# Cross-attention scores computed once with queries on partitions, tiles normalised by GpSimd and turned by TensorE transposes

## The reference

```python
q_r = jnp.einsum('bshq,hqr->bhsr', q_big, W_qr)
k_r = jnp.einsum('bld,hdr->bhlr', kv_rope, W_kr)
scores = jnp.einsum('bhsr,bhlr->bhsl', q_r, k_r)
attn = jax.nn.softmax(scores, axis=-1)
ctx_c = jnp.einsum('bhsl,bld->bhsd', attn, kv_rope)
ctx_lat = jnp.einsum('bhsd,hkd->bshk', ctx_c, w_kc_kv)
out = ctx_lat.reshape(b, s, H * K) @ Wo.T
```

## Time and profile before

| | |
|---|---|
| Median of three executions | 260.71 us (259.54 to 261.23) |
| The profiled execution | 261.54 us, of which the span of instructions is 259.4 us |
| Granted TensorE clock, mean | 0.983 |
| PE busy | 239.6 us, 92% of the span, 1563 matmuls |
| DVE busy | 196.5 us, 76% |
| ACT busy | 132.2 us, 51% |
| POOL busy | 103.3 us, 40% |
| Chain that ended last | PE 71%, DVE 13%, DMA 5%, ACT 4% |
| HBM read, written | 14.43 MB, 0.52 MB |

### The profile page before, as it was taken

How to read it: one execution, slowest core, us unless ns; L and a number is a source line. 1 busy time by engine, 2 the same in 40 slices (tenths; PEclk the granted TensorE clock), 3 DMA queues, 4 the chain that set the end, 5 groups by cost and what they waited for, 6 DMA issues and landing times.

```text
span 259.4 us, 4344 instructions
## 1 busy us (share of the span) xinstructions
PE 239.6 (92%) x1563; PEld 171.6 (66%) x1563; DVE 196.5 (76%) x351; ACT 132.2 (51%) x285; POOL 103.3 (40%) x135
## 2 busy tenths in 40 slices
PE   7999999988997799998999999999999999989971
PEld 4478797754654457675666767677776777668850
DVE  1377577899765899869889998986669895897574
ACT  1545377566368366556467656654435533313430
POOL 7297400000114307745466555556255533001362
PEclk9999999999999899999999999999999999999995
DMA  6999940000000840000000000000000000000011
GB/s 246 321 278 322 412 167 0 4 1 3 0 3 0 158 86 0 3 0 0 5 0 0 3 0 0 0 3 0 0 3 0 1 3 1 0 3 0 1 40 40
DMA packets 4500, 13.65 MB, mean 53 GB/s; under 512 B 512, under 2 KB 1280, under 8 KB 4352
## 3 DMA queue, kind: packets, MB, share of 16 engines
q1 hardware_dynamic: 4048, 11.29, 13.1%
q0 software_dynamic: 432, 2.10, 3.7%
HBM read 14.43 MB, written 0.52 MB: 58 GB/s over the span
## 4 chain that ended last, share of the span: by engine, by line
PE 71%; DVE 13%; DMA 5%; ACT 4%; issue 2%; SPq 2%; POOL 1%; POOLq 0%; DVEq 0%; ACTq 0%
PE ps L844 11%; PE ps L794 7%; PE ps L821 5%; PE ps L858 5%; PE ps L822 5%; PE ps L795 5%; PE ps L778 5%; DMA wq<-in_wq 5%; PE ps L634 3%; PE ps L923 3%; DVE mneg L1350 3%; PE ps L831 2%; PE ps L696 2%; PE ps L681 2%; PE ps L574 2%
## 5 line engine op out<-in xcount | busy, mean ns | idle before, releaser
L1184 ACT ACTIVATE probs<-ps 128x512 f32<-128x512 f32 x64 | 38.0, 597 | 46.7 <-PE ps L822 45.8
L1412 DVE TENSOR_REDUCE xmneg<-ps 128x1 f32<-128x512 f32 x64 | 43.0, 688 | 16.2 <-PE ps L795 15.8
L445 POOL TENSOR_TENSOR psums<-psums,probs 128x512 f32<-128x512 f32 x30 | 38.6, 1288 | 10.8 <-ACT probs L1184 8.3
L441 POOL TENSOR_TENSOR psums<-probs 128x512 f32<-128x512 f32 x15 | 19.2, 1281 | 43.1 <-ACT probs L1184 43.1
L794 PE MATMUL ps<-KA,QA 128*128 128x512 f32 x64 | 30.3, 474 | 2.8 <-DVE xmneg L1412 1.9
L844 PE MATMUL ps<-probs,kv_dup 128*64 128x256 f32 x256 | 31.2, 385 | 0.0
L1430 DVE RECIPROCAL xrcp<-ps 128x256 f32<-128x256 f32 x16 | 28.0, 1751 | 1.9 <-PE ps L831 1.9
L1176 ACT ACTIVATE QA<-ps 64x256 fp32r<-64x256 f32 x64 | 24.2, 378 | 10.1 <-PE ps L778 8.9
L1350 DVE TENSOR_REDUCE mneg<-ps 128x4 f32<-128x1024 f32 x16 | 19.6, 1224 | 9.4 <-PE ps L574 9.0
L821 PE MATMUL ps<-QA,KA 128*128 128x512 f32 x64 | 26.0, 406 | 0.0
L398 POOL TENSOR_TENSOR rstd<-mv,eps_col 128x1 f32<-128x1 f32 x12 | 2.3, 189 | 59.4 <-DVE mv L1338 59.1
(11 more groups left out here) (162 smaller groups left out, 459.7 us busy)
## 6 DMA issues: line engine op xcount, KB each, us to landing
wu<-in_wu SPq DMA_DIRECT2D x4, 640.0 KB, 8.9
wq<-in_wq SPq DMA_DIRECT2D x4, 512.0 KB, 13.4
wcT<-in_wcT SPq DMA_DIRECT2D x4, 384.0 KB, 12.3
wE<-in_wE SPq DMA_DIRECT2D x4, 320.0 KB, 11.2
w13T<-in_w POOLq DMA_DIRECT2D x1, 1024.0 KB, 8.2
x1T<-in_xT SPq DMA_DIRECT2D x1, 512.0 KB, 3.7
kvp<-in_kv POOLq DMA_DIRECT2D x1, 512.0 KB, 6.1
x_nat<-in_xn SPq DMA_DIRECT2D x1, 512.0 KB, 18.6
```

Of the source, the lines that this page charges most:

```text
L445: g.tensor_tensor(psums[:, s, :], psums[:, s, :], probs[:, s, kc, :], ALU.add).then_inc(xadd_sb, 1)
L1184: a.activation(probs[:, n % 2, kc, :], ps[:, 2 + u % 2, :], ACT.Exp).then_inc(xexp_sb, 1)
L1412: v.tensor_reduce(xmneg[:, n % 4, qt, hh:hh + 1], ps[:, u % 2, :], AX.X, ALU.max, negate=True).then_inc(xmax_sb, 1)
```

## The change

The scores are computed once, with queries on partitions. `xscores(n, r)` takes the place of both `xmax` and `xexp` on PE and uses banks 0, 1 and 2 in turn. DVE reduces each tile to its negated maximum as before; ACT then applies the exponential to the same tile with that maximum as a bias per partition, and gives the sum of each row as a second output (`xsum`). DVE takes the reciprocal of two columns of sums at a time, and POOL multiplies each 128x512 tile by it in place (`xnorm`, four per unit). PE transposes the tiles, four transposes of 128x128 for each block of keys (`xturn(t)`, t = 4m + kc, seven steps behind the scores: `OFF` = 7), into bank 3 for even t and bank 5 for odd t. ACT copies the even ones out of PSUM and DVE the odd ones, into `PT`, which lies where `probs` was. `xpv(m)` then runs all its eight matmuls in one piece, two iterations behind the scores, and DVE copies the result to `ctxn` (`context`). The sums by POOL, the matmul with ones, the split and transpose of the maxima, the rows they were copied to and the blanking of them are gone. The loop has still 18 iterations; `query(n + 2)` now stands in step r = 0. `routing(0)` moves behind the copies of step r = 2 of iteration 16. The diff, cut to its core (the new side mostly, since what is removed is described above):

```diff
+NQ = 3
+OFF = 7
+
+
+def score_bank(u):
+    return u % 2 if u < 4 else (u - 2) % 3
+
+
+LAST_IN_BANK = [max([w for w in range(u) if score_bank(w) == score_bank(u)], default=-1) for u in range(4 * NUNIT)]
...
+        PT = probs[:].rearrange("p s k q -> p (s k) q")
...
+        xmneg = sb("xmneg", [P, 3, 4], scope=late)
+        xsum = sb("xsum", [P, 3, 4], scope=late)
+        xrcp = sb("xrcp", [P, 3, 4], scope=late)
+        xp = sb("xp", [P, 3, 4, LK], scope=late)
...
+            pool.wait_ge(rstd_sb[0], 2)
+            g.memset(QB[DC:DC + 4].bitcast(F32), 0.0).then_inc(qzero, 1)
+            pool.wait_ge(qzero, 1)
...
+            def xnorm(n, r):
+                pool.wait_ge(xrcp_sb, 2 * n + r // 2 + 1)
+                g.tensor_scalar(xp[:, n % 3, r, :], xp[:, n % 3, r, :], xrcp[:, n % 3, r:r + 1], None, ALU.mult).then_inc(xnorm_sb, 1)
+
+            pool.wait_ge(const2, 2)
+            for n in range(NUNIT):
+                if n in (4, 5):
+                    reciprocal_root(0, n - 2)
+                if n in (NE + 5, NE + 6):
+                    reciprocal_root(1, n - NE - 5)
+                for r in range(4):
+                    xnorm(n, r)
...
-            def xmax(n, r):
+            def xscores(n, r):
                 b = n // NPAIR
                 hh, qt = r // 2, r % 2
                 u = 4 * n + r
                 s = n % NQ
                 if r == 0:
-                    pe.wait_ge(qzero, n + 1)
                     pe.wait_ge(qhi_sb, 4 * n + 4)
                     pe.wait_ge(qlo_sb, 2 * n + 2)
-                if u >= 2:
-                    pe.wait_ge(xmax_sb, u - 1)
...
+                if u == 0:
+                    pe.wait_ge(qzero, 1)
+                if u == 4:
+                    pe.wait_ge(exp_sb, 4 * NGRP)
+                if LAST_IN_BANK[u] >= 0:
+                    pe.wait_ge(xexp_sb, LAST_IN_BANK[u] + 1)
                 q = slice(qt * P, qt * P + P)
-                o = bank(u % 2)
+                o = bank(score_bank(u))
                 pe.matmul(o, QA[:, s, hh, q], KA[:, b * LK:(b + 1) * LK], start=True, stop=False)
...
+                pe.matmul(o, QB[:, s, hh, q], KB[:, b * LK:(b + 1) * LK], start=False, stop=True).then_inc(xs_ps, 1)
...
+            def xturn(t):
+
+                m, kc = t // 4, t % 4
                 if kc == 0:
-                    pe.wait_ge(xm_sb, 2 * n + 2)
-                if u == 0:
-                    pe.wait_ge(exp_sb, 4 * NGRP)
-                if u >= 2:
-                    pe.wait_ge(xexp_sb, u - 1)
-                k0 = b * LK + kc * P
-                o = bank(2 + u % 2)
-                pe.matmul(o, KA[:, k0:k0 + P], QA[:, s, :, :], start=True, stop=False)
-                pe.matmul(o, KB[:, k0:k0 + P], QB[:, s, :, :], start=False, stop=True).then_inc(xexp_ps, 1)
-
-            def xsum(n):
-
-                if n == NUNIT - 1:
-                    pe.wait_ge(xlast_sb, NKC - 1)
+                    pe.wait_ge(xnorm_sb, 4 * m + 4)
+                if t >= 2:
+                    pe.wait_ge(xT_dve if t % 2 else xT_act, t // 2)
+                for r in range(4):
+                    mm = pe.transpose(ps[:, 3 + 2 * (t % 2), r * P:(r + 1) * P], xp[:, m % 3, r, kc * P:(kc + 1) * P], ident[:])
+                mm.then_inc(xT_ps, 1)
+
+            def xpv(m):
...
+                b = m // NPAIR
+                pe.wait_ge(xT_act, 2 * m + 2)
+                pe.wait_ge(xT_dve, 2 * m + 2)
+                if m == 0:
+                    pe.wait_ge(sums_sb, NGRP)
                 else:
-                    pe.wait_ge(xadd_sb, 3 * n + 3)
-                for hh in range(2):
...
+                    pe.wait_ge(ctxn_sb, m)
+                for kc in range(NKC):
+                    for hh in range(2):
+                        mm = pe.matmul(ps[DC * hh:DC * hh + DC, 4, 0:SEQ], kv_dup[:, NKC * b + kc, 0, :],
+                                       PT[:, (4 * m + kc) % 8, hh * SEQ:(hh + 1) * SEQ], start=(kc == 0), stop=(kc == NKC - 1))
+                mm.then_inc(xpv_done, 1)
...
+                    t = 4 * n + r - OFF
...
                     if n < NUNIT:
-                        xmax(n, r)
-                    if LAG <= n < NUNIT + LAG:
-                        xexp(n - LAG, r)
-
+                        xscores(n, r)
+                    if r == 0 and n + 2 < NUNIT:
+                        query(n + 2)
...
+                    if n == NUNIT and r in (1, 2):
+                        for p in (2 * r - 2, 2 * r - 1):
+                            out_proj(2, p)
+                            out_proj(3, p)
+                    if n == NUNIT and r == 3:
+                        out_proj(2, 4)
+                        out_proj(3, 4)
                         gates_T(0, ps[:, 7, 0:SEQ])
-                    if n == NUNIT and r == 3:
+                    if n == NUNIT + 1 and r == 0:
+                        out_proj(2, 5)
+                        out_proj(3, 5)
                         spread_gates(0, 0)
                     if n == NUNIT + 1 and r == 1:
-                        out_proj(2, 4)
-                        out_proj(3, 4)
                         spread_gates(0, 1)
+                    if n == NUNIT + 1 and r == 2:
+                        out_proj(2, 6)
+                        out_proj(3, 6)
                     if n == NUNIT + 1 and r == 3:
-                        out_proj(2, 5)
-                        out_proj(3, 5)
                         spread_gates(0, 2)
...
+                    if r == 3 and n >= 2:
+                        xpv(n - 2)
+                    if 0 <= t < 4 * NUNIT:
+                        xturn(t)
+            up(0)
             spread_gates(0, 3)
-            for kc in range(NKC):
-                xpv(NUNIT - 1, kc)
-            xsum(NUNIT - 1)
-            out_proj(2, 6)
-            out_proj(3, 6)
-            up(0)
-            pe.wait_ge(xexp_sb, NKC * NUNIT)
...
+            def xexp(u):
+                n, r = u // 4, u % 4
+                act.wait_ge(xmax_sb, u + 1)
+                if r == 0 and n >= 3:
+                    act.wait_ge(xT_ps, 4 * (n - 2))
+                a.activation(xp[:, n % 3, r, :], ps[:, score_bank(u), :], ACT.Exp, bias=xmneg[:, n % 3, r:r + 1],
+                             accum_out=xsum[:, n % 3, r:r + 1]).then_inc(xexp_sb, 1)
+
+            def xturn(t):
+                act.wait_ge(xT_ps, t + 1)
+                if t == 0:
+                    act.wait_ge(pv_done, NGRP)
+                if t % 4 == 0 and t >= 8:
+                    act.wait_ge(xpv_done, t // 4 - 1)
+                a.activation(PT[:, t % 8, :], ps[:, 3, :], ACT.Copy).then_inc(xT_act, 1)
...
+                    u = 4 * n + r
+                    if 1 <= u <= 4 * NUNIT:
+                        xexp(u - 1)
...
+                    if r == 0 and n + 2 < NUNIT:
                         query_hi(n + 2)
...
+                    if n == NUNIT and r == 3:
                         gates_T(0, ps[:, 7, 0:SEQ])
+                    t = u - OFF
+                    if 0 <= t < 4 * NUNIT and t % 2 == 0:
+                        xturn(t)
...
-                hh, qt = r // 2, r % 2
...
+                dve.wait_ge(xs_ps, u + 1)
+                v.tensor_reduce(xmneg[:, n % 3, r:r + 1], ps[:, score_bank(u), :], AX.X, ALU.max, negate=True).then_inc(xmax_sb, 1)
+
+            def xrecip(n, k):
+                dve.wait_ge(xexp_sb, 4 * n + 2 * k + 2)
+                v.reciprocal(xrcp[:, n % 3, 2 * k:2 * k + 2], xsum[:, n % 3, 2 * k:2 * k + 2]).then_inc(xrcp_sb, 1)
+
+            def xturn(t):
+                dve.wait_ge(xT_ps, t + 1)
+                if t == 1:
+                    dve.wait_ge(pv_done, NGRP)
+                if t % 4 == 1 and t >= 8:
+                    dve.wait_ge(xpv_done, t // 4 - 1)
+                v.tensor_copy(PT[:, t % 8, :], ps[:, 5, :]).then_inc(xT_dve, 1)
+
+            def context(m):
+                b, p = m // NPAIR, m % NPAIR
+                dve.wait_ge(xpv_done, m + 1)
+                v.tensor_copy(ctxn[:, p, b * SEQ:(b + 1) * SEQ], ps[:, 4, 0:SEQ]).then_inc(ctxn_sb, 1)
...
+            for n in range(NUNIT + 2):
+                for r in range(4):
+                    t = 4 * n + r - OFF
+                    if n < NUNIT:
+                        xmax(n, r)
+                    if r == 0 and n >= 3:
+                        context(n - 3)
+                    if r == 0 and n in (NE + 5, NE + 6):
+                        norm_stats(1, n - NE - 5, ps[:, 7, 0:SEQ], x1)
+                    if r == 1 and 1 <= n <= NUNIT:
+                        xrecip(n - 1, 1)
+                    if r == 3 and n < NUNIT:
+                        xrecip(n, 0)
+                    if 0 <= t < 4 * NUNIT and t % 2 == 1:
+                        xturn(t)
+                    if r == 2 and n < 3:
+                        attn_norm(NGRP - 3 + n)
+                    if r == 2 and n in (4, 5):
+                        norm_apply(0, n - 2, x1)
+                    if r == 2 and n in (NE + 5, NE + 6):
```

(13 more changed lines are left out.)

230 lines of the change are left out of this document (23 added, 207 removed).

## The result

The change makes the kernel slower, and by more than forecast. The median goes from 260.91 us (259.54 to 261.23, four executions) to 281.41 us (280.06 to 283.28, four executions); the ratio is 1.081 with a 95% interval of 1.077 to 1.085. The prediction was 265 us, with a range that ended at 270.

What follows compares the result with a forecast made beforehand. The prediction took a PE-DVE loop to bound full units at 8.0 us against 7.42. Its stretches, +4.5 - 1.6 + 3.5 - 2.0 + 0.4 - 0.7, gave +4.1 and a median of 265 us, range 258.5 to 270.

Steps and rivals of the forecast that it cites:

- the loop: Units of the main loop: PE and DVE wait for each other once a unit, 8.0 us against 7.42 before.
- the small reciprocal: DVE's reciprocal of 128x2 sums: taken as 0.20 us, between 0.17 and 1.10.
- the exponential: ACT's exponential with bias column and row sum: taken as 0.87 us in all, range 0.68 to 1.28.
- PE's saving: PE's own work per unit about 1.1 us below 7.42; comes through in units 12 and 13, -2.0 us.
- the wait at `gates_T`: After unit 16 starts, `gates_T` waits for `routing(0)` on DVE behind the copy of step 2: 2.4 us stall.
- Rivals 1, 2 and 3: PE-DVE loop shorter, 260 us (chance 0.16); loop doesn't close, 252 us (0.05); loop longer, 269 us (0.13).
- rival 4: PE's clock falls to 0.50 in the loop, if transposes don't count as busy: above 315 us, chance 0.04.
- rival 5: POOL becomes the bound: at 2.5 us a multiplication a unit is 10 us, near 289 us, chance 0.04.
- Step 1: POOL's new multiplications: 0.9 us each, 3.6 a unit, 5.1 at worst, bounded by 0.61 and 1.28.
- one of the prediction's own signs of being wrong: Wrong if PE waits for POOL ahead of transposes or the exponential ahead of a tile, copies are short, or clock falls.
- Step 2: POOL's second-half multiplications, released about 3.5 us, needed by transposes at 7.5: each may take 1.9 before PE waits.
- Step 3: PE's clock in the loop: expected 1.00 at 85% busy, with a chance of 0.04 for a fall.

## Why the prediction was wrong in size

**What it had right.** The direction, and the loop. Units 6 to 11 were forecast at 48.0 and took 47.93, of which the five from 7 to 11 are 7.90 each. That the two sums agree to 0.1 is luck, since unit 6 began at the lower clock and took 8.43; in the runs without that dip the six take 47.4. Piece by piece the loop fits: from a unit's start DVE's first copy begins at 2.05 (forecast 1.97), `xpv` at 5.61 (5.73), and the next unit at 7.90 (8.04). PE idles ahead of `xpv`, DVE runs without a gap from copy to copy and idles during `xpv`; `query_lo` moved by one step took 0.78 off the unit, of its 0.86. The copy of 512 columns (0.66 taken) is 0.69 as a record and 0.60 from one start to the next, the small reciprocal 0.16, the exponential in range, though shorter than taken. Units 12 and 13, where PE's saving comes through, 19.97 for 19.6; the wait at `gates_T` 2.02 for 2.4. Rivals 1, 2 and 3 are out by the same rows, rival 4's rule by the filler of transposes, and rival 5 since POOL is 6.25 busy in a unit of 7.90, whose length did not change when its multiplications were halved.

**Step 1 that failed: "POOL loses three additions and gains four multiplications ... I take 0.9, 3.6 a unit, 5.1 at worst."** It is 1.56, 6.25 a unit, outside the range of 0.61 to 1.28. The bounds were a cast of one input and an addition of two, on the thought that a multiplication by a column reads one tile and lies between them. It lies above both. With 1.04 instead (the other form) the time is 8.9 lower, and units 0 to 2 come out at 24.16 for the forecast 24.1, without the 2.3 that the first transposes waited in unit 1. Part of that agreement is the clock of these units in that execution (0.93), which comes and goes. That PE waits for POOL ahead of the transposes was one of the prediction's own signs of being wrong, and it came.

**Step 2 that failed: "each of the two may take up to 1.9 before PE waits."** The slack was worked out for the transposes alone. By that measure 1.56 was safe, and for the transposes of units 7 to 11 it was. But POOL's queue also holds `reciprocal_root`, four times in the loop, and behind it wait `norm_apply` on DVE and `normed_T` on PE. In units 5 and 14 it stood behind multiplications of which the last two were released only by a reciprocal of step 1. The prediction put 8.3 and 8.2 on these units; they took 13.28 and 12.76, and 8.73 and 8.63 once `reciprocal_root` was placed two multiplications earlier. That edit gave 9.5 us. The two failures overlap: each repair alone is worth about 9, and both act on the same stalls. Without this step a price within the range would not have given 272.5: units 5 and 14 make 4.8 of the 6.0 us by which that run's span is over the forecast one. No run has these two repairs and nothing else.

**Step 3 that failed: "I expect 1.00" for the clock, with 0.04 for a fall.** It did stay at 1.00 in units 7 to 11, where PE was busy 6.9 of 7.90 us, and transposes did no harm. It fell behind the idle stretches of units 5 and 14, and with work issued into the stalls of 3.5 and 4.1 us the units took 2.4 and 1.5 us less (and unit 6 another 0.5). Rival 4 was the right engine and the wrong cause: it asked only whether the loop's steady share was enough, and not what a single long wait costs on top of itself.

**What stays open.** Units 0 to 2 took 28.24 in the profiled execution, of which 2.3 is the wait for POOL. Up to 2 more come and go between executions with the clock of that stretch (0.76 to 0.94), and no run here says with what. Nor does one say why the clock fell behind a wait of 1.95 and not behind one of 2.11. The 0.8 at the start is the memset, by the one profile with it cut.

## What to carry to other kernels

When work is added to an engine with idle time, list everything that stands behind it in that engine's queue and who waits for it, not only the consumer of the new work; here a helper of two operations and 0.8 us, standing behind 6.3 and 3.1 us of new work, put 9.5 us on the path, while the same new work cost nothing in units 7 to 11. A wait of several microseconds on TensorE can cost more than its length, so price it with the slow matmuls behind it, and look for a place a step earlier for what releases it. When two engines hand work back and forth once a unit, a lighter unit brings nothing until the order in the loop is opened: the same arithmetic went from 281.4 to 259.7 us by orders and one form of instruction, which is where the kernel stood before the change.

## What the runs showed of the hardware

- POOL's multiplication of fp32 by a column, 128x512: 1563 ns as TENSOR_SCALAR, 1039 ns as TENSOR_TENSOR with the column broadcast, against 1281 ns for an addition of two full tiles. With 926 ns for 256 columns the first form costs 2.49 ns a column and 0.29 us fixed. The Trainium skill, "GPSIMD Engine Reference", section 4.1, calls one-input operations roughly line-rate beside VectorE and two-input ones about twice as slow; here the form with one tile as input was the slowest of the three.
- Behind an idle 3.5 us PE's matmuls ran at the lower level of its clock: 3.68 us for an `xpv` of 1.95. Matmuls and transposes issued into the idle time kept it at 1.00 alike. Behind shorter waits it went either way: it fell behind 1.95, 2.80 and 2.97 us, and did not behind 1.30, 1.45 and 2.11 us.
- A sum written by the exponential is a second record of 202 ns on ACT, behind an exponential of 0.69 us whose own length does not change (685 ns without it). It moves the next operation by only about 0.1 us (0.66 to 0.68 behind the exponential's start, 0.57 to 0.59 without the sum).
- Two normalising operations of DVE that took 0.73 us with POOL idle took 1.89 while POOL blanked 1536 elements in each of only four partitions (1.37 us), and 1.03 while it blanked 512 (0.52 us).
